# The square of the distance from the centre: two ScalarE activations a step become two GpSimd products

## What is computed

```python
v = group_norm(x, 32 groups)
y = spectral_conv2d(v, w1, w2) + einsum(v, conv_w) + conv_b     # 16 + 16 x 16 Fourier modes
for layer in (1, 2):                                            # 64 -> 64 channels, per point
    y = silu(y) @ base_w.T + b_splines(y, grid) @ (spline_w * scaler)   # 8 cubic basis functions
out = x + gelu(y)
```

## Time and profile before

| | |
|---|---|
| median of three runs | 3723.7 us |
| the three runs | 3718.49, 3725.59, 3723.7 us |
| profiled execution, span from first to last instruction | 3720.9 us |
| its own time | not recorded apart from the span |
| TensorE matmul busy | 3646.5 us (98%) |
| VectorE busy | 3531.2 us (95%) |
| ScalarE busy | 3374.6 us (91%) |
| GpSimd busy | 110.0 us (3%) |
| 128x1024 instructions on ScalarE: offset, square | 1280, 256 |
| `cube` and `inner_cube` instructions on VectorE | 2816 |

### The profile page before, as it was taken

The page is one execution under the profiler, slowest core; times in us unless marked ns, Lnnn a source line. Parts: engine busy times, 40 slices in busy tenths (PEclk is TensorE's granted clock), DMA queues, the critical chain, the costliest instruction groups (busy, mean ns, idle before and its releaser), DMA issues.

```text
span 3720.9 us, 101035 instructions
## 1 busy us (share of the span) xinstructions
PE 3646.5 (98%) x37676; PEld 1471.8 (40%) x37676; DVE 3531.2 (95%) x3917; ACT 3374.6 (91%) x3509; POOL 110.0 (3%) x131
## 2 busy tenths in 40 slices
PE   8987999999999999999999999999999999999998
PEld 4555533333333333333333333333333333333333
DVE  8874999999999999999999999999999999999997
ACT  4422999999999999999999999999999999999997
POOL 0000000000000000000000000000000000000000
PEclk9998999999999999999999999999999999999999
DMA  9997133323222222232222222223222222222221
GB/s 314 326 225 155 45 98 117 113 79 97 66 63 73 56 72 67 61 73 60 69 68 61 73 63 66 71 57 73 65 63 73 55 73 67 61 73 59 70 68 52
DMA packets 256583, 329.34 MB, mean 89 GB/s; under 512 B 86768, under 2 KB 185712, under 8 KB 254448
## 3 DMA queue, kind: packets, MB, share of 16 engines
q1 hardware_dynamic: 235648, 257.29, 24.1%
q0 software_dynamic: 18288, 66.59, 10.2%
q10 hardware_dynamic: 2560, 4.20, 0.5%
HBM read 239.91 MB, written 88.08 MB: 88 GB/s over the span
## 4 chain that ended last, share of the span: by engine, by line
PE 89%; DVE 1%; issue 1%; ACT 0%; DMA 0%; SPq 0%; DVEq 0%; ACTq 0%
PE l_ps L1100 82%; PE y_ps L1087 3%; PE y_ps L1079 3%; PE inv_ps L1115 1%; PE inv_ps L1100 0%; ACT offset L1021 0%; DMA inv_h_sb<-inv_h_dram 0%; PE l_ps L1115 0%; DVE cube3r L957 0%; ACT size L1017 0%; DVE cube1r L957 0%; DVE cube2l L957 0%; ACT below L1014 0%; DVE cube1l L957 0%; DVE cube0r L957 0%
## 5 line engine op out<-in xcount | busy, mean ns | idle before, releaser
L1021 ACT ACTIVATE offset<-size 128x1024 f32<-128x1024 f32 x1280 | 1240.6, 1044 | 8.1
L957 DVE SCALAR_TENSOR_TENSOR cube0r<-below,offset 128x1024 f32<-128x1024 f32 x256 | 313.7, 1225 | 83.0 <-ACT offset L1021 79.1
L966 DVE SCALAR_TENSOR_TENSOR inner_cube<-below,square 128x1024 f32<-128x1024 f32 x256 | 313.8, 1226 | 0.0
L957 DVE SCALAR_TENSOR_TENSOR cube4l<-above,offset 128x1024 f32<-128x1024 f32 x256 | 313.7, 1225 | 0.0
L957 DVE SCALAR_TENSOR_TENSOR cube2r<-below,offset 128x1024 f32<-128x1024 f32 x256 | 313.2, 1223 | 0.5
L957 DVE SCALAR_TENSOR_TENSOR cube3l<-above,offset 128x1024 f32<-128x1024 f32 x256 | 313.5, 1225 | 0.0
L957 DVE SCALAR_TENSOR_TENSOR cube4r<-below,offset 128x1024 f32<-128x1024 f32 x256 | 313.4, 1224 | 0.0
L957 DVE SCALAR_TENSOR_TENSOR cube3r<-below,offset 128x1024 f32<-128x1024 f32 x256 | 313.3, 1224 | 0.0
L957 DVE SCALAR_TENSOR_TENSOR cube2l<-above,offset 128x1024 f32<-128x1024 f32 x256 | 313.2, 1223 | 0.0
L957 DVE SCALAR_TENSOR_TENSOR cube1l<-above,offset 128x1024 f32<-128x1024 f32 x256 | 313.0, 1223 | 0.0
L957 DVE SCALAR_TENSOR_TENSOR cube1r<-below,offset 128x1024 f32<-128x1024 f32 x256 | 312.9, 1222 | 0.0
(11 more groups left out here) (160 smaller groups left out, 5911.9 us busy)
## 6 DMA issues: line engine op xcount, KB each, us to landing
big<-in_x_dram SPq DMA_DIRECT2D x128, 512.0 KB, 8.3
x_ring<-in_x_dram SPq DMA_DIRECT2D x256, 256.0 KB, 4.1
out_dram<-act_out SPq DMA_DIRECT2D x128, 512.0 KB, 2.7
act_out<-in_x_dram POOLq DMA_DIRECT2D x127, 512.0 KB, 7.2
rows_t<-rows_scratch SPq DMA_DIRECT2D x512, 32.0 KB, 5.2
rows_scratch<-rows SPq DMA_DIRECT2D x14, 1024.0 KB, 5.8
big<-in_spec_w_r_dram SPq DMA_DIRECT2D x16, 512.0 KB, 11.7
big<-in_spec_w_i_dram SPq DMA_DIRECT2D x16, 512.0 KB, 12.2
```

The costliest lines, as they stand in the source:

```text
L957: nc.vector.scalar_tensor_tensor(out=cube[q][side][:], in0=distance[layer][:], scalar=EDGE - KNOTS[q], in1=offset[layer][q][:], op0=ALU.mi ...
L966: nc.vector.scalar_tensor_tensor(out=inner_cube[:], in0=below[layer][:], scalar=EDGE, in1=square[layer][:], op0=ALU.subtract, op1=ALU.mult ...
L1021: nc.scalar.activation(offset[layer][q][:], size[layer][:], ACT.Square, bias=-KNOTS[q]).then_inc(offset_ready[layer], 1)
```

## The change

ScalarE no longer makes `square`. GpSimd makes it as a product of `size` with itself, once for each layer and tile. As `size` now has a reader on another engine, ScalarE waits, before it writes `size` again, for the square of the tile before. GpSimd's loop is written anew, since the products of different tiles lie around the DMAs that add x: the first four products stand ahead of the loop, one turn of the loop holds the add of tile i - 1, the product of layer 1 of tile i and that of layer 0 of tile i + 2, and the rest stands behind it. The wait of `cube_of_x` on VectorE for `square_ready` stays as it was and now waits for GpSimd.

```diff
         @block.gpsimd
         def _(pool):
-            with pool.Fori(0, TILES - 1) as j:
+            def add_x(j):
                 pool.wait_ge(gelu_ready, j + 1)
                 pool.sem_inc(seen_by_pool, 1)
                 pool.dma_start(act_out[:], tile_in_dram(x, *place(j)[:2]), accum_op=ALU.add).then_inc(x_added, 16)
+
+            def square_of(layer, tile):
+
+                pool.wait_ge(size_ready[layer], tile + 1)
+                pool.sem_inc(seen_by_pool, 1)
+                nc.gpsimd.tensor_tensor(square[layer][:], size[layer][:], size[layer][:],
+                                        ALU.mult).then_inc(square_ready[layer], 1)
+
+            square_of(0, 0)
+            square_of(0, 1)
+            square_of(1, 0)
+            square_of(0, 2)
+            with pool.Fori(1, TILES - 2) as i:
+                add_x(i - 1)
+                square_of(1, i)
+                square_of(0, i + 2)
+            add_x(TILES - 3)
+            square_of(1, TILES - 2)
+            square_of(1, TILES - 1)
+            add_x(TILES - 2)
...
                 act.wait_ge(below_ready[layer], tile + 1)
+                if like >= 1:
+
+                    act.wait_ge(square_ready[layer], tile)
                 nc.scalar.activation(size[layer][:], below[layer][:], ACT.Abs, bias=EDGE,
                                      scale=-1.0).then_inc(size_ready[layer], 1)
                 act.wait_ge(size_ready[layer], tile + 1)
                 for q in range(NK):
                     nc.scalar.activation(offset[layer][q][:], size[layer][:], ACT.Square,
                                          bias=-KNOTS[q]).then_inc(offset_ready[layer], 1)
-                nc.scalar.activation(square[layer][:], size[layer][:], ACT.Square).then_inc(square_ready[layer], 1)
```

## The result

| | before | after |
|---|---|---|
| median | 3724.14 us (4 runs) | 4155.6 us (4 runs, 4155.44 to 4155.76) |
| ratio | | 1.1159, 95% interval 1.1146 to 1.1172 |
| span of the profiled execution | 3720.9 us | 4153.5 us (its own time 4155.51) |

What follows compares the result with a forecast made beforehand. TensorE was taken to bound the kernel at 25.77 us a step, VectorE close behind at 25.47. 256 products at 2.18 us make 558, less 58 idle: +500 on 3723.7 gives 4224 us, range 3900 to 4350.

Steps and rivals of the forecast that it cites:

- The bound: Before the change TensorE bounds at 25.77 us a step; VectorE's work is 25.47, leaving it 58.4 us spare in all.
- ScalarE's two squares at 0: Removing ScalarE's two squares frees 1.9 us a step, 243 us of ScalarE time, but gains 0 on the path.
- its new wait at 0: ScalarE's wait before `size` for the previous tile's square costs 0, with over 20 us to spare.
- d: Time each GpSimd product takes from VectorE: 2.18 us, two operand reads (2.09) plus 0.09 lost overlap.
- The sum: VectorE's step becomes 29.83 us; 256 x 2.18 = 558, less 58 idle, gives +500 us, so 4224 us.
- Who waits for whom does not change the sum: Whether GpSimd gets in first or VectorE stands idle at `inner_cube` while the product runs, VectorE loses about 2.18 us.
- What would show it: Expected signs: steps of 29.8 us, two longer VectorE instructions or 2 us idle before `inner_cube`, TensorE near 86%, clock 1.00.
- rival 1: GpSimd reads beside VectorE without slowing it; time stays at 3724 us, 3722 at best; chance 0.12.
- GpSimd's queue at 0: Two products in GpSimd's queue with the add of x cost 0; the store has 15 us against 2.9 late.
- Code loading at 0: One-time code loading ahead of GpSimd's first product costs 0, covered by 12.8 us before the first `inner_cube`.
- TensorE's clock: TensorE's clock stays at full, 1.00, despite standstills of 2.2 us a product; any slowing would mostly be hidden.

Runs made afterwards that it cites:

- the last run: Against the changed kernel: ScalarE makes the square again, GpSimd multiplies fixed weights into an unread tile, no engine waits for its products; 4185.6 us.

## Why the prediction was right

- **The bound.** That VectorE was 0.30 us a step behind TensorE, 58 us in all, and would take over, is shown: 55.9 us come out when TensorE is relieved before the change, and none after it.
- **ScalarE's two squares at 0, and its new wait at 0.** Shown by the fill that reads nothing, which keeps every wait and lets ScalarE off its squares: ratio 0.9996.
- **d.** The term was 2.18 us, two operands through one reader at 1.04 each and 0.09 for the lost overlap. Measured are 2.04 in the steady steps (2.09 if VectorE's step is taken as 25.38 us), and one operand costs 0.85 where two cost 1.72, half the columns 0.86. The build-up by operands was right, the reader quicker than ScalarE's (0.85 us for 1024 columns), and no overlap is lost on top. That 2.18 came as near as it did is in part luck: two products at 1.72 would be 3.44 us a step, and the 4.18 measured hold 0.72 of the DMA's issue, which the prediction had at 0.
- **The sum.** 500 us were forecast, 431.5 came: a term mis-sized by 14%. The 58 us of idle time were nearly right (cube0r's idle went from 83.0 to 30.0 us, with 5.4 new before `inner_cube`). VectorE's balance closes: 481.7 of longer instructions, less 53.0 idle before `cube0r`, plus 5.4, make 434. The 558 us of the forecast were too many by 256 x 0.14 = 36 for d itself, and by 28 x (2.04 - 1.09) = 27 for the products that got in beside the 28 PSUM copies of the inverse transform, a cover that the prediction did not see: 558 - 63 - 58 = 437.
- **"Who waits for whom does not change the sum"** is the step that failed, though it did no harm to the number. It named two ways, GpSimd first or VectorE never letting it in, and the kernel took a third: in by the preparation. And the price is not the same everywhere: 1.73 for one product at a preparation, 4.18 for two with the DMA's issue between them, 1.74 each with VectorE standing, 1.09 beside a PSUM copy, and, in the run with one operand, 2.75 us of standing for an instruction that costs 0.85 at the COPY.
- **What would show it** was half right: steps of 29.8 us (29.56 measured) and TensorE waiting for VectorE, but no longer cube in the steady steps and no wait before `inner_cube`, and TensorE busy for 92% in place of 86. Cubes that keep 1.22 us beside a product were named as the sign of rival 1; they kept it, and the loss was there all the same.
- **GpSimd's queue at 0** held for the store and the gelu, since the adds are issued right behind the first product (2002.74). It did not hold for VectorE, which stands for 0.72 us a step of that issue. The run in which nobody waits shows how thin the first part is.
- **Code loading at 0** held: `size` of the first tile ends at 361.92 us, the first product starts at 362.18 and takes 1.88.
- **TensorE's clock** was forecast at 1.00, and was 0.95 to 0.97 of 2.4 GHz in the long stretches (0.969 over the run). After 1.91 us idle two groups of matmuls took about twice their length:

```profile
2006.88 1.09 PE L1122 MATMUL l_ps<-cube3r,turned_w 64*64 64x512 f32 x8 [1.91 <-DVE cube3r L977]
2008.02 1.99 PE L1122 MATMUL l_ps<-cube3l,turned_w 64*64 64x512 f32 x8
2009.75 1.89 PE L1122 MATMUL l_ps<-cube4r,turned_w 64*64 64x512 f32 x8
```

From 2006 to 2012 us the granted clock was 0.72, between the levels of 1.2 and 2.4 GHz; a step later, after 1.60 us idle, it was 1.00. Shown to cost nothing: without the `bowl` matmuls the time is the same.

The rule of the Trainium skill that spoke against the change (SBUF — State Buffer, "Who interferes with whom") agrees with the runs on who collides: reads of GpSimd against two-operand instructions of VectorE, and nothing beside those for an instruction that only writes. That the second one waits out the whole of the other does not hold for every instruction here: with one operand, GpSimd's lasts 2.76 us at the least and costs the COPY 0.85. The COPY ends at 2018.53, GpSimd's instruction goes on until 2020.24, and the cubes beside it keep their 1.21 us. The estimate for the length, 2.25 us from the Trainium skill's GPSIMD Engine Reference, 3.1 (its figure is for an add), is longer than the 1.88 us that the first product shows; the sum by it, 4264 us, is farther off than the one from the rows. That the COPY and TENSOR_SCALAR wait too, which read one tile from SBUF, also agrees with SBUF — State Buffer: it counts these among the instructions that can take the shared pair in a two-port mode. No run here shows their mode itself.

## What to carry to other kernels

Before moving elementwise work to an idle GpSimd, count VectorE's slack per step and look at the operands: beside a VectorE that is full of instructions with two SBUF operands, a GpSimd instruction costs VectorE at least the time of all its reads, about 0.85 us per operand of 128x1024 float32 here, and relief for ScalarE is worth nothing if ScalarE does not bound. Work that only writes was free, and reads were free for as long as they ran beside a VectorE instruction that reads PSUM. Keep DMAs that someone waits for out of a queue that can be starved, and out of the place just ahead of a GpSimd product.

None of the runs beat the kernel before with the whole work done. TensorE bounds it, and only leaving a matrix product out made it faster.

## What was not expected of the hardware

- In the steady steps a row of two-operand VectorE instructions did not give way: a product of 1.88 us was recorded for 15.28 us in the changed kernel and for 26.83 in the last run, without one cube longer than usual meanwhile. It is no law. In the last steps of the changed kernel a product issued at 4082.77 got in between two such instructions with no idle time ahead, and `cube2r` took 2.91 us. In the run with the product into a tile that nobody reads, one got in behind the first cube after 4.12 us of idle time, in every second step. Why there and not elsewhere stays open.
- A GpSimd product right behind a DMA's issue holds VectorE's TENSOR_SCALAR from before the issue is over: 0.72 us of issue and 1.93 of product make the 2.71 of that one instruction, within 0.06.
- VectorE instructions of 128x2 and 128x64 elements took 1.88 and up to 2.73 us, longer than a cube of 128x1024. A long mean on a tiny instruction (1299 ns for 128x64) is the mark of this collision in the table of groups; the cubes show little (`cube4r` a mean of 1335 ns, from the 28 early ones).
- GpSimd's TENSOR_SCALAR of one operand takes at the least 2.76 us and its TENSOR_TENSOR of two 1.88, yet VectorE pays 0.85 and 1.72 at the COPY. How long GpSimd is busy does not tell what VectorE loses.
- The recorded length of a GpSimd instruction holds the time it was kept out: 8181 ns mean, 1.88 us alone.
